# Where the late query and key chunks of a 32-wide attention are projected: ring of three PSUM banks or the context's bank

## What is computed

```
layer 0: q = x Wq, k = ctx Wk, v = ctx Wv; 32 heads of 16 columns, 8 key/value heads; softmax; Wo; layer norm
layer 1: attention of x with itself, 16 heads of 32 columns; scores * mask - 10000 (1 - mask); softmax; Wo
         then cross attention to ctx in the same form, 16 heads of 32 columns
         then a gelu MLP of width 2048
layers 2 and 3: recurrent (rwkv) blocks
```

```
scores = einsum('bhqd,bhkd->bhqk', q, k) / sqrt(32)
scores = scores * mask - 10000.0 * (1.0 - mask)
out    = einsum('bhqk,bhkd->bhqd', softmax(scores), v)
```

## Times and profile before

| | us |
|---|---|
| median of 3 runs | 4241.41 |
| lowest and highest of them | 4233.95, 4247.2 |
| profiled execution, its own time | 4250.26 |
| its span, first to last instruction | 4248.5 |
| its mean granted TensorE clock | 0.948 |

### The profile page before, as it was taken

How to read it: one execution, slowest core, us unless ns; L and a number is a source line. 1 busy time by engine, 2 the same in 40 slices (tenths; PEclk the granted TensorE clock), 3 DMA queues, 4 the chain that set the end, 5 groups by cost and what they waited for, 6 DMA issues and landing times. The chain is left out here.

```text
span 4248.5 us, 66434 instructions
## 1 busy us (share of the span) xinstructions
PE 3740.6 (88%) x24448; PEld 2278.7 (54%) x24448; DVE 2618.1 (62%) x5675; ACT 2156.9 (51%) x4272; POOL 1669.7 (39%) x1865
## 2 busy tenths in 40 slices
PE   7988899898888989989888998998988889899898
PEld 4544565545545456555554545655555454565555
DVE  5765646666576564566657656456665765646665
ACT  5655733434666573343366657334336675733433
POOL 4554542232454454223245444422324544542222
PEclk9999999899999999999989999999999999999899
DMA  4032211102204222010220322101022032220102
GB/s 135 15 107 64 81 69 41 59 21 100 75 15 122 55 83 71 32 59 31 90 76 26 108 65 75 69 31 59 31 90 77 27 108 65 75 69 31 59 32 98
DMA packets 94558, 276.11 MB, mean 65 GB/s; under 512 B 25472, under 2 KB 25984, under 8 KB 73088
## 3 DMA queue, kind: packets, MB, share of 16 engines
q1 hardware_dynamic: 94208, 271.58, 19.8%
HBM read 201.24 MB, written 4.19 MB: 48 GB/s over the span
## 5 line engine op out<-in xcount | busy, mean ns | idle before, releaser
L805 POOL TENSOR_SCALAR probs<-probs,row_inv 128x512 f32<-128x512 f32 x1024 | 693.1, 693 | 643.9 <-DVE row_inv L720 643.9
L664 ACT ACTIVATE probs<-probs,row_max 128x512 f32<-128x512 f32 x1024 | 733.1, 725 | 130.8 <-DVE row_max L736 129.6
L559 PE MATMUL ps<-ident,probs 128*128 128x128 f32 x4096 | 609.8, 291 | 170.6 <-ACT pT L658 144.3
L559 PEld LDWEIGHTS ps<-ident,probs 128*128 128x128 f32 x4096 | 481.2, 147 | 381.1 <-ACT pT L658 206.9
L658 ACT ACTIVATE pT<-ps 128x512 f32<-128x512 f32 x768 | 429.8, 602 | 113.2 <-PE ps L559 112.7
L369 PE MATMUL ps<-mix,wring 128*128 128x512 f32 x1024 | 471.0, 596 | 3.5 <-DMA wring<-in_blocks_dram 3.4
L534 PE MATMUL ps<-kstack,qstack 96*128 96x512 f32 (+1 forms) x1024 | 383.4, 469 | 16.7 <-DMA qstack<-hi 7.1
L736 DVE CUSTOM_DVE_ANT_0 probs<-ps,maskA 128x512 f32<-128x512 f32 x512 | 329.3, 681 | 43.9 <-PE ps L534 43.9
L736 DVE CUSTOM_DVE_ANT_0 probs<-ps,neg 128x512 f32<-128x512 f32 x512 | 340.5, 685 | 8.9
L369 PEld LDWEIGHTS ps<-mix,wring 128*128 128x128 f32 x1024 | 191.2, 190 | 198.7 <-issue 179.3
L1532 POOL TENSOR_TENSOR hinv<-hvar,minus_half 128x32 f32<-128x32 f32 x24 | 146.2, 6092 | 377.3 <-DVE hvar L1254 377.3
(11 more groups left out here) (177 smaller groups left out, 7056.4 us busy)
## 6 DMA issues: line engine op xcount, KB each, us to landing
wring<-in_blocks_dram SPq DMA_DIRECT2D x151, 1024.0 KB, 5.0
qstack<-hi SPq DMA_DIRECT2D x256, 64.0 KB, 2.0
kstack<-hi SPq DMA_DIRECT2D x256, 64.0 KB, 2.0
maskA<-in_mask_dram SPq DMA_DIRECT2D x9, 1024.0 KB, 7.4
rows<-in_rows_dram SPq DMA_DIRECT2D x8, 1024.0 KB, 4.6
qstack<-hi SPq DMA_DIRECT2D x256, 32.0 KB, 2.0
qstack<-lo SPq DMA_DIRECT2D x128, 64.0 KB, 2.0
kstack<-lo SPq DMA_DIRECT2D x128, 64.0 KB, 2.0
```

Source lines behind the costliest of these rows:

```text
L559: ins = nc.tensor.transpose(tile[:, qc * P:(qc + 1) * P], probs[:, m % PSLOTS, qc, kc * P:(kc + 1) * P], ident[:, :])
L664: nc.scalar.activation(p, p, ACT.Exp, bias=row_max[:, n % PSLOTS, qc:qc + 1], scale=-1.0, accum_out=row_sum[:, n % PSLOTS, qc:qc + 1]).the ...
L805: nc.gpsimd.tensor_scalar(p, p, row_inv[:, (n - 1) % PSLOTS, qc:qc + 1], 1.0, ALU.mult, ALU.mult)\
```

## The change

In the 32-wide attentions the chunks q2, k2, q3 and k3 no longer take a bank of the ring. They are all projected into bank 7, `OBANK`, which no context uses before n = 6. Since all four use one bank, each waits until the one before it has been emptied by ScalarE (`BEFORE`): q2 waits for nothing, k2 for q2, q3 for k2, k3 for q3. The first context, at n = 6, waits until k3 has been emptied. `act_split` reads the bank that `project_bank` names. The ring then holds only transposes in the head loop. No instruction that computes is added or removed.

```diff
+        BEFORE = {('q', 2): None, ('k', 2): ('q', 2), ('q', 3): ('k', 2), ('k', 3): ('q', 3)}
...
+        def in_heads(A, kind, g):
+            return not A.shared and g >= 2
+
+        def project_bank(A, kind, g):
+            return OBANK if in_heads(A, kind, g) else ring.bank(*((kind, A.tag) if kind == 'k' and A.shared else (kind, A.tag, g)))
+
+        def project_tile(pe, A, kind, g):
+
+            if not in_heads(A, kind, g):
+                return take(pe, *((kind, A.tag) if kind == 'k' and A.shared else (kind, A.tag, g)))
+            if BEFORE[kind, g] is not None:
+                before, b = BEFORE[kind, g]
+                pe.wait_ge(*(dve_emptied if before == 'v' else act_emptied).when(before, A.tag, b))
+            return ps[:, OBANK, :]
+
         def pe_q(pe, A, g, fcs=range(C), tile=None, ready=None):
-            tile = take(pe, 'q', A.tag, g) if tile is None else tile
+            tile = project_tile(pe, A, 'q', g) if tile is None else tile
...
         def pe_k(pe, A, g, fcs=range(C), tile=None, ready=None):
             label = ('k', A.tag) if A.shared else ('k', A.tag, g)
-            tile = take(pe, *label) if tile is None else tile
+            tile = project_tile(pe, A, 'k', g) if tile is None else tile
...
                             if kc == 0:
+                                if vg == 0 and not A.shared:
+                                    pe.wait_ge(*act_emptied.when('k', t, 3))
...
-            nc.scalar.activation(split[:, s, :], ps[:, ring.bank(*label), :], ACT.Identity, bias=bias,
+            nc.scalar.activation(split[:, s, :], ps[:, project_bank(A, kind, g), :], ACT.Identity, bias=bias,
```

## The result

The median of 10 runs is 4273.34 us (4244.68 to 4282.46), that of the kernel before, 10 runs on the same chips, 4239.48 (4225.02 to 4248.84). The ratio is 1.0069, with a 95% interval of 1.0047 to 1.0091: **the change makes the kernel 0.7% slower**, some 29 us. The profiled execution took 4265.88 us with a span of 4264.1, 15.6 us more than the one before.

The account below looks back on a forecast made before the run. The prediction held that an attention's end moves only with the start of the context in turn 6. Eight attentions losing 1.87 us each, 15.0 us, on the median of 4241.41 gave 4256.4 us, range 4241 to 4270.

Parts of the forecast that it names:

- What binds: Heads of an attention: only the start of the context in turn 6 moves the attention's end.
- (a): Turn 0: q2 no longer waits for an earlier values tile; TensorE had no gap there, worth 0.
- (b): Third transpose of head 0: its 1.02 us wait for k2's split goes, worth 0.
- (d): Turn 4: q3 waits for k2's split, which is over since turn 1, worth 0.
- (c): Turn 1: k2 newly waits for q2's split and starts 2.66 us later, holding VectorE up 1.49 us.
- rival C: TensorE's new gaps may draw a clock fall into 284 to 298: 27.0 us lost, 4268.4 us; chance 0.13.
- It passes on: ScalarE, full from turn 1's delay to 284.2, makes q3's split 1.49 us later too.
- (e): Turn 5: head 3's first transposes lose their 1.22 us wait; k3 waits for q3's split instead, 0.87 us gained.
- (f): Turn 6: the context newly waits for k3's split and starts 1.87 us later, or 0.38 without turn 1's delay.
- The restart price of 0.06 us: TensorE's added delay after a wait, read from transposes, entering three times; bounded by 0 and 0.56 us elsewhere.
- main sum: All eight 32-wide attentions lose 1.87 us each, 15.0 us in all; chance 0.62.
- Rival B: Ring waits bind and both new waits are free: 15.1 us gained, 4226.3 us; chance 0.05.

Follow-up runs that it names:

- the matched pair: Three 8-column matmuls per attention added in turn 1, in the kernel before and in the change: 4211.96 us and 4236.01 us.
- the second experiment: Only q2 and k2 put into bank 7, q3 and k3 in the ring, against the kernel before: 4260.24 us, ratio 1.0044.
- the control: The change plus three 8-column matmuls ahead of k2's first half in turn 1, against the kernel before: 4236.01 us, ratio 0.9995.

## Why the prediction was right, and where its size was off

**What binds**: right. The end of an attention follows the context in turn 6: that started 292.42 - 255.32 = 37.10 us behind the first L762, against 33.55 before, 3.55 us later, and the last reciprocal is 3.56 us later. From the start of that context to the last L762 it is 50.16 or 50.17 us in all eight attentions after the change, and 50.15 to 50.17 in seven of the eight before (51.31 in the other).

**(a), (b)**: worth nothing, as said; for (a) the kernel with k2 back in the ring shows it, with turn 1 at 7.59 to 7.60 us as before, for (b) the pair q2 and k2 alone. **(d)**: no wait seen.

**(c), the step that failed in size.** Worked out were 1.49 us. With the clock up it was 9.12 - 7.60 = 1.52 us. With the clock down, as in seven of eight attentions, it was 2.3 to 3.2. I had the fall of the clock as rival C, but looked for it in the stretch from 284 to 298, on the ground that TensorE has no slack there. That was the wrong question: cover must be counted at the lower clock too. The k2 half and the scores behind it had 1.17 us of cover, and the wait had used it up. Half and scores at the lower level cost up to 1.66 us more (10.78 - 9.12), and all of it went through.

**It passes on**: right. Turn 1's delay of 3.19 us in A1 came out at the end as 3.56, the difference of 0.37 being that of (e) and (f). ScalarE's split of q3 stands 29.69 us behind the first L762, not 26.50: here it is after the change, with k3's.

```profile
285.01 0.72 ACT L643 ACTIVATE split<-ps,scaled 128x512 f32<-128x512 f32 x1
...
291.70 0.67 ACT L643 ACTIVATE split<-ps,cols 128x512 f32<-128x512 f32 x1
```

**(e) and (f)**: right to the hundredth, 0.38 us, shown alone with k2 back in the ring. The restart price of 0.06 us, of which I was least sure, held only in sum. Behind the wait of A2 the row after the half starts 409.18 - 407.76 = 1.42 us after it, where it was 262.34 - 261.02 = 1.32 without a wait: 0.10 for a projection. The transposes behind the context start 294.28 - 292.42 = 1.86 us after it, and 289.74 - 287.88 = 1.86 with q2 and q3 alone, where no wait stands ahead: nothing for the context. Twice 0.10 and once 0 is 0.20, where three times 0.06 had been taken, which is luck.

**The sum.** 8 x 1.87 = 15.0 us was the price without the clock; the heads measured 25.1, or 3.1 for each attention, and not all eight alike, as had been foretold: 86.67 to 87.30 us. Rival C's 27.0 us is nearer to this than the main sum, but it too is partly luck: it priced the right cause, at much the right size, in a stretch where the clock never fell. That the two profiled executions differ by 15.6 us is chance, not confirmation: 25.1 in the heads less 9.5 outside. The timed runs, 29 us, agree with the heads. Since the place of instructions can move the time by as much, and the change moves waits within TensorE's program, the 24 us of the matched pair (both with the small matmuls) are the better evidence that it is the heads that cost. The range's upper end, made of C and the restart prices, was short of the plain median by 3 us.

**Rival B** named the point from which the change would gain, the split ahead of the exponentials. Moved there, the change does gain, but so does the kernel before with the same move (0.9965 and 0.9969), so it is the split's place that gains and not bank 7. The page Perfetto Trace Analysis of the Trainium skill asks in Matmul Optimizations that all eight banks be used; by these runs an idle bank is worth 0.2 us for an attention when the split stands early and costs 3.1 when it stands late. The rule of its section Optimizing Tensor Performance, that matmul groups rotate through banks, is what the change broke for q2 and k2, and the second experiment has its price: 22.0 us in the heads.

## What to carry over

Before two tiles are put in one bank, look where in its turn the engine that empties the first does so: a split that is queued behind four exponentials makes the second tile wait for all of them. Here moving the split was the remedy, and worth 0.3% by itself. Count the cover of a new TensorE wait with the clock at its lower level, since the wait itself may bring it down. Compare profiles by the stage that was changed, not by the span; and when a stage that wasn't changed moves, try a control that adds the same instructions without their work.

## What the runs showed of the hardware

The clock of TensorE often fell within 1.5 us of the end of a wait of 2.4 us: in seven of the eight attentions of the kernel after, and in none of eight when the wait was filled with matmuls. With the gap open the window from 262 to 265 us had 0.57 in the change and 0.51 in the control, where three small matmuls left 1.87 us of the wait; filled it had 1.00. A fall there cost up to 1.66 us.

Where instructions stand in TensorE's program moved the time by more than the change did. Three matmuls of 8 columns in turn 1 of each attention, ahead of the recurrent blocks, made the kernel before 0.6% faster (0.9942); the same behind them, nothing (1.0004). The waits that moved coincide with 16 KB packets of an instruction queue: of those over 1 us (1.1 to 2.2), 119 in 123. A difference of half a per cent between two versions of this kernel can have this cause alone, and then says nothing of the edit.
